# A decoder layer on one core: the FFN unit's steps within a slot, and who makes x1 at the end

## What is computed

```python
x = x + attn(ln(x))      # 32 query heads, 8 key/value heads of 128, rope, causal softmax;
                         # q, k, v, o weights are (codes - 8) * scales, scales per 128 rows
q1 = clip(round(ln(x) / s1 + z1), 0, 255) - z1          # fake_quant, times s1
q2 = clip(round(ctx / s2 + z2), 0, 255) - z2            # ctx: 2 x 1024 x 1024, times s2
x = x + (q1 @ q2) * (s1 * s2)
bw = mean(|w|, row) * sign(w) - clip(w, -1, 1) + clip(w, -1, 1)   # in this order, 1024 x 1024
x = x + ln(x) @ bw.T
```

## Time and profile before

| | |
|---|---|
| runs | 1189.84, 1192.79, 1192.4 us; median 1192.4 |
| profiled execution | 1189.75 us, its span 1188.0 us |
| busy | PE 1111.0 (94%), DVE 925.9 (78%), ACT 656.9 (55%), POOL 594.1 us (50%) |
| mean granted TensorE clock | 0.986 |
| chain that ended last | PE 82%, DVE 11%, issue 2%, ACT 2% |

### The profile page before, as it was taken

The page is one execution under the profiler, slowest core; times in us unless marked ns, Lnnn a source line. Parts: engine busy times, 40 slices in busy tenths (PEclk is TensorE's granted clock), DMA queues, the critical chain, the costliest instruction groups (busy, mean ns, idle before and its releaser), DMA issues.

```text
span 1188.0 us, 19387 instructions
## 1 busy us (share of the span) xinstructions
PE 1111.0 (94%) x5924; PEld 552.8 (47%) x5924; DVE 925.9 (78%) x1491; ACT 656.9 (55%) x1454; POOL 594.1 (50%) x692
## 2 busy tenths in 40 slices
PE   3799999789999999999999999999999998769998
PEld 2334444345545445545544545444454453435553
DVE  6867531358988878888888888999999988788773
ACT  2344432466677767767767776666666664223320
POOL 0112000477676766767767677776777765200000
PEclk9999999999999999999999999999999999899999
DMA  7344552176766757667576676666767754600111
GB/s 252 107 126 119 177 149 82 27 153 146 159 151 145 166 127 158 149 139 164 139 158 145 144 165 130 153 145 148 150 146 143 161 108 95 179 1 19 35 38 52
DMA packets 283186, 152.94 MB, mean 129 GB/s; under 512 B 229216, under 2 KB 241760, under 8 KB 283104
## 3 DMA queue, kind: packets, MB, share of 16 engines
q1 hardware_dynamic: 275328, 138.60, 50.3%
q10 hardware_dynamic: 7776, 13.37, 4.0%
HBM read 93.19 MB, written 4.19 MB: 82 GB/s over the span
## 4 chain that ended last, share of the span: by engine, by line
PE 82%; DVE 11%; issue 2%; ACT 2%; DMA 1%; POOL 1%; SPq 0%; ACTq 0%; DVEq 0%; POOLq 0%
PE side_ps L523 9%; PE side_ps L525 9%; PE side_ps L524 9%; PE proj_ps L655 8%; PE out_ps L655 8%; PE side_ps L634 7%; PE proj_ps L523 6%; PE proj_ps L524 6%; PE proj_ps L525 6%; PE score_ps L617 2%; PE score_ps L620 2%; PE score_ps L621 2%; PE score_ps L766 2%; DVE x_acc L1386 2%; DVE x_acc L1395 1%
## 5 line engine op out<-in xcount | busy, mean ns | idle before, releaser
L523 PE MATMUL side_ps<-hT,w_a 128*128 128x512 f16 x512 | 195.7, 382 | 13.5 <-DVE rot L1311 13.5
L1110 POOL TENSOR_TENSOR w_b<-prob,w_b 128x896 f16<-128x896 f32 (+2 forms) x192 | 188.6, 996 | 37.2 <-ACT w_b L942 37.2
L1098 POOL TENSOR_TENSOR swapped<-swapped,sin_t 128x512 f32<-128x512 f32 x80 | 102.1, 1276 | 194.2 <-ACT swapped L857 194.2
L524 PE MATMUL side_ps<-hT,w_a 128*128 128x512 f16 x512 | 195.4, 382 | 0.0
L525 PE MATMUL side_ps<-hT,w_a 128*128 128x512 f16 x512 | 195.3, 381 | 0.0
L1386 DVE SCALAR_TENSOR_TENSOR x_acc<-proj_ps,o_now,x_acc 128x1024 f32<-128x1024 f32 x116 | 148.0, 1276 | 53.2 <-PE proj_ps L655 53.2
L1103 POOL TENSOR_SCALAR prob<-prob,row_inv 128x512 f32<-128x512 f32 (+3 forms) x256 | 170.8, 678 | 17.7 <-DVE row_inv L1468 10.9
L915 ACT ACTIVATE prob<-score_ps,neg_max 128x512 f32<-128x512 f32 (+3 forms) x256 | 132.2, 519 | 60.6 <-DVE neg_max L1361 27.1
L1117 POOL TENSOR_TENSOR q_sb<-rot,q_sb 128x512 f16<-128x512 f32 x64 | 74.1, 1158 | 173.1 <-ACT q_sb L907 173.1
L1386 DVE SCALAR_TENSOR_TENSOR x_acc<-out_ps,o_now,x_acc 128x1024 f32<-128x1024 f32 x116 | 147.4, 1271 | 0.0
L942 ACT ACTIVATE w_b<-prob 128x896 f16<-128x896 f32 (+2 forms) x192 | 99.6, 552 | 54.6 <-POOL prob L1103 49.9
(11 more groups left out here) (188 smaller groups left out, 2140.0 us busy)
## 6 DMA issues: line engine op xcount, KB each, us to landing
stage_c<-in_codes_dram SPq DMA_DIRECT2D x96, 256.0 KB, 2.8
stage_s<-in_scales_dram SPq DMA_DIRECT2D x96, 256.0 KB, 3.8
stage_o<-in_codes_dram SPq DMA_DIRECT2D x64, 256.0 KB, 3.8
ctx_raw<-in_ctx_dram ACTq DMA_DIRECT2D x32, 256.0 KB, 3.3
x_acc<-in_x_dram SPq DMA_DIRECT2D x8, 512.0 KB, 9.3
prob<-in_ffn_w_dram ACTq DMA_DIRECT2D x16, 256.0 KB, 2.9
work<-w_b SPq DMA_TRANSPOSE x256, 3.0
hT<-in_x_dram SPq DMA_DIRECT2D x8, 512.0 KB, 5.1
```

The lines of the kernel that those rows point to most:

```text
L523: pe.matmul(o, stat(0), mov(0), start=first, stop=False)
L524: pe.matmul(o, stat(0), mov(1), start=False, stop=False)
L1098: pool.tensor_tensor(swapped[:, :], swapped[:, :], sin_t[:, :], ALU.mult).then_inc(done, 1)
L1110: ins = pool.tensor_tensor(prob16[:, 1, to:to + w], prob[:, at:at + w], prob16[:, 0, to:to + w], ALU.subtract)
```

## The change

Four edits.

1. In every slot with an FFN unit, `wf_clip` goes ahead of `q_lo` and `norm` on GpSimd, `wf_sign` ahead of `prob_split` part 0 on ScalarE, and `wf_difference` between `o_add` 1 and `o_add` 2 on VectorE.
2. Slot 62 is now an ordinary slot. Head 30's eight units all stand in slot 63 as `o_unit` and `o_add`; only head 31 has `two_units` and `add_two`. ScalarE runs part 1 of `prob_split` and `o_cut` ahead of `ao_part` in slot 63.
3. The column parts go to ScalarE (Identity with scale and bias, a new column of `scal`). Tile 0's x1 is still added from PSUM by VectorE, and its stats and root run alone. Tiles 1 to 7 are copied from PSUM by ScalarE (`y_copy`) and added to the input by GpSimd (`x1_add`). The transposes of tiles 4 and 5 stand between `turn_i1(0)` and `cross(0)`, those of 6 and 7 behind it.
4. Clip and rounding of tiles 2 to 7 leave VectorE: GpSimd clips (`x1_clip`), ScalarE adds the rounding constant (`x1_round`), and `x1_sum` takes it off again.

```diff
@@ TensorE, slot
-                if known(p) and p == N_SLOTS - 2:
+                if known(p) and p == N_SLOTS - 1:
                     scores(p, i, g, 0)
                     o_unit(p - 1, prev[1], 3)
                     scores(p, i, g, 1)
                     o_unit(p, i, 0)
+                    o_unit(p, i, 1)
                     scores(p, i, g, 2)
-                    for k in range(1, UNITS):
-                        o_unit(p, i, k)
+                    o_unit(p, i, 2)
+                    o_unit(p, i, 3)
                     for k in range(UNITS):
-                        two_units(NH - 2, 0, k)
-                    weigh(p - 1, prev[1], prev[0])
-                    return
-                if known(p) and p == N_SLOTS - 1:
-                    for u in range(3):
-                        scores(p, i, g, u)
-                        two_units(NH - 2, 1, u)
-                    two_units(NH - 2, 1, 3)
+                        o_unit(N_SLOTS, 0, k)
                     column_sums(0, 0)
                     weigh(p - 1, prev[1], prev[0])
                     return
@@ TensorE, the end
             for k in range(UNITS):
-                two_units(NH - 1, 1, k)
-            for t in range(TB, TT):
-                turn_y(t)
+                two_units(1, k)
             turn_i1(0)
+            turn_y(4)
+            turn_y(5)
             cross(0)
+            turn_y(6)
+            turn_y(7)
@@ ScalarE, slot
+                if known(p) and wf_early(p) is not None:
+                    wf_sign(wf_early(p))
                 prob_split(p, 0)
...
                 if has_ahead:
                     q_swap(p + Q_AHEAD)
-                if known(p) and wf_early(p) is not None:
-                    wf_sign(wf_early(p))
+                if known(p) and p == N_SLOTS - 1:
+                    prob_split(p, 1)
+                    o_cut(p, i)
+                    column_part(0, 0)
+                    ao_part(p - 1, i - 1)
+                    return
@@ ScalarE, new steps
+            def column_part(b, h):
+
+                act.wait_ge(col_summed, b * NB + h + 1)
+                act.activation(cc[:, b, h * S:(h + 1) * S], col_ps(b, h), ACT.Identity, scale=scal[:, 6:7],
+                               bias=scal[:, 10:11]).then_inc(cc_ready, 1)
+
+            def y_copy(t):
+
+                act.wait_ge(y_turned, t + 1)
+                act.activation(x1_rows(t), o_banks[t % 2][:, :, :].rearrange("p h (k t) -> p (h k) t", t=P), ACT.Copy)\
+                    .then_inc(y_copied, 1)
+
+            def x1_round(t):
+
+                act.wait_ge(x1_clipped, t - 1)
+                act.activation(xn[t % 2], xn[t % 2], ACT.Copy, bias=ROUND).then_inc(x1_rounded, 1)
@@ ScalarE, the FFN loop
                 if more:
                     x1_scale(t + 2)
+                if more:
+                    x1_round(t + 2)
                 if t:
                     h3_part(t)
@@ GpSimd, slot
+                    if known(p) and wf_early(p) is not None:
+                        wf_clip(wf_early(p))
                     if not (known(p) and p >= N_SLOTS - 1):
                         pool.wait_ge(q_done, p + 1)
                         q_lo(p + 1)
...
-                    if known(p) and wf_early(p) is not None:
-                        wf_clip(wf_early(p))
@@ GpSimd, the end
+            def x1_add(t):
+
+                pool.wait_ge(y_copied, t)
+                pool.wait_ge(xs_landed[t], 16)
+                pool.tensor_tensor(x1_rows(t), x1_rows(t), by_block(xs[:, t, :]), ALU.add).then_inc(x1_ready, 1)
+
+            def x1_clip(t):
+
+                pool.wait_ge(x1_scaled, t + 1)
+                pool.tensor_scalar(xn[t % 2], xn[t % 2], QMAX, 0.0, ALU.min, ALU.max).then_inc(x1_clipped, 1)
+
+            for t in range(1, 4):
+                x1_add(t)
+            for t in range(4, TT):
+                x1_add(t)
+                x1_clip(t - 2)
+            x1_clip(TT - 2)
+            x1_clip(TT - 1)
@@ VectorE, slot
                 if has_o:
                     o_add(p, i, 1)
+                if known(p) and wf_early(p) is not None:
+                    wf_difference(wf_early(p))
+                if has_o:
                     o_add(p, i, 2)
                 if has_ahead:
                     q_cos(p + Q_AHEAD)
-                if known(p) and wf_early(p) is not None:
-                    wf_difference(wf_early(p))
@@ VectorE, the FFN loop
                 if t:
                     y_part(t - 1, 0)
-                if more:
-                    x1_quant(t + 2)
```

More of the change, by code:

```diff
@@ L338, in build @@
         y_turned = sem("y_turned")
+        x1_first = sem("x1_first")
+        y_copied = sem("y_copied")
         x1_ready = sem("x1_ready")
@@ L1070, in _ @@
             wf_upper(WF_UNITS - 1)
-            next_roots(2)
+            column_part(0, 1)
+            column_part(1, 0)
+            y_copy(1)
+            next_roots(1)
+            y_copy(2)
+            y_copy(3)
             ao_part(N_SLOTS - 1, SLOTS - 1)
             x1_scale(0)
+            column_part(1, 1)
+            x1_sum(0)
+            next_roots(1)
             x1_scale(1)
-            x1_sum(0)
+            i1_T_part(0)
             x1_sum(1)
-            i1_T_part(0)
+            for t in range(TB, TT):
+                y_copy(t)
             i1_T_part(1)
@@ L1370, in o_scales @@
                 if last is not None:
-                    j, of = NH - 1 + last, (NKV - 1, RF - 2 + last)
+                    j, of = last, (NKV - 1, RF - 1)
                 dve.tensor_copy(o_now[:, of[1] % 2, :],
@@ L1413, in slot @@
                 n = p + FIRST_PIECES
-                if known(p) and p == N_SLOTS - 2:
-                    j = o_scales(g, i, 0)
+                if known(p) and p == N_SLOTS - 1:
+                    j = o_scales(g, i)
                     maxima(p, i, 0)
-                    q_sum(p + 1)
                     o_add(p - 1, i - 1, 3)
                     maxima(p, i, 1)
+                    dve.wait_ge(o_now_ready, j)
                     o_add(p, i, 0)
```

121 lines of the change are left out of this document (51 added, 70 removed).

## The result

| | before | changed |
|---|---|---|
| runs | 1189.84 to 1192.79; median 1191.4 us | 1173.84 to 1176.75; median 1175.6 us |
| ratio to before | | 0.9866, 95% interval 0.9846 to 0.9886 |
| profiled execution, its span | 1189.75, 1188.0 us | 1173.84, 1172.0 us |
| busy PE, DVE, ACT, POOL | 1111.0, 925.9, 656.9, 594.1 us | 1106.4, 904.1, 671.7, 621.7 us |

The change makes the kernel faster by 15.8 us; the prediction said 13.0 and 1179.4 us. Of the 3.8 us between 1179.4 and 1175.6, 1.0 is the base: the forecast started from the median of three runs, 1192.4, and with the fourth it is 1191.4. The sign, the sum of the end and the ceiling of the FFN stage were right. The slots gave more than their terms, and the experiments show that most of it came with GpSimd's clip, a move that the prediction had priced at nothing.

The account below looks back on a forecast made before the run. TensorE was taken as the bound, with 34.6 us of idling as the ceiling. FFN slots 3.6, first slots 1.2, end 8.2 and FFN stage 0 sum to 13.0 us, from 1192.4 to 1179.4 us; range 1173.5 to 1188.

Parts of the forecast that it names:

- The three stretches: First eight slots, FFN slots, and last two slots to first FFN product: idle TensorE of 6.5, 4.1 and 24.0 us.
- FFN slots, 3.6 us: Slots with an FFN unit: TensorE's nine waits for q_sum, together 4.0 us, go nearly wholly, gaining 3.6 us.
- The difference in the idle time ahead of o_add 2: FFN slots: VectorE's wf_difference, 0.94 us, fills 0.97 us of idling, so the next q_sum comes 0.4 us earlier.
- First slots, 1.2 us: First slots: slot 1's q_sum starts 0.8 us earlier and one more 0.43 us wait goes; bounds 0 and 3.
- The end, 8.2 us: Last two slots to the first FFN product: turn_h3(0) at 1058.7 instead of 1066.87, 8.2 us earlier.
- The table load: Ahead of tile 0's root on ScalarE: load now waits behind y_copy(1) and adds 1.28 us before the root.
- GpSimd's clip, taken at 1.85 us: FFN stage: GpSimd's clip of 1024 elements takes 1.85 us, between 1.44 and 2.52, and just fits.
- rival (a): FFN stage: a slow GpSimd clip makes it wait 0.6 us a tile, giving 1182.4 us; chance 0.15.
- The FFN stage at nothing: FFN stage: TensorE still bounds it and the new clip and rounding chain just fits, costing 0.
- (b): Slots: the moves give nothing because ao_part or the sine becomes the next wait, giving 1184.2 us; chance 0.14.
- (c): End: ScalarE's extra copies knot the queues, 8.2 us shrink to 1 or 2, giving 1185.6 to 1186.6; chance 0.08.
- (d): Slots: the early sign waits for a late wf_lower and slows the kernel; 1.85 us delay gives 1196; chance 0.03.

Follow-up runs that it names:

- e10: The kernel before with only GpSimd's clip moved ahead of q_lo and the norms: 1184.1 us, ratio 0.9948.
- e6: The changed kernel with three of GpSimd's x1 adds held back by waits: 1172.5 us, ratio 0.985.
- e12: The changed kernel with the old order of clip, sign and difference in every slot, and slot 63's difference behind the last o_add: 1185.4 us, ratio 0.9953.
- e2: The kernel before with only the slots' new order of clip, sign and difference: 1181.9 us, ratio 0.9923.
- e11: The kernel before with only ScalarE's sign moved ahead of prob_split: 1202.8 us, ratio 1.0107.

## Why the prediction was right, and where not

- **What bounds, and the ceiling.** The three stretches named from the earlier trace rows are those that got shorter, and nothing else did. Of the 34.6 us of idle TensorE, 12.9 went by the same rows (1.8, 4.1 and 7.0). The gain is larger than that, since an idle time listed between pipelined matmuls is shorter than what the wait costs; the next point has the numbers.
- **FFN slots, 3.6 us: the term was too small, and the named move the smaller part.** 6.7 us were measured. Two steps failed. The first is the price of a wait. The nine listed waits were priced at their listed 0.44 us; but a matmul is shown as 0.38 us long and follows its forerunner after 0.22, so each listed wait hides 0.16 more. By the starts of the slots, the nine slots with a wait are 0.6 to 0.7 us longer than in the changed kernel, 5.5 us together. The other slots from 40 on are longer by up to 0.2 without a listed wait, 0.6 us in sum, and another 0.6 lies between slot 7 and slot 40. The second is where the waits came from. The slots alternated between 12.71 and 12.17 us, in the trace of before, and now take 12.115 each; the prediction did not ask for the difference between the two kinds. Its step "GpSimd's clip moves ahead of q_lo ... Both cost nothing" was true of the cost and blind to the gain (e10: 5.6 us).
- **The difference in the idle time ahead of o_add 2** did what was said: it stands straight behind o_add 1, at 0.47 us instead of 0.94, as GpSimd's sine no longer runs beside it, and ao_rest waits for ao_part as forecast. On top of the early clip it is worth 1.2 us, since behind that TensorE is nearly the bound already.

```profile
831.05 0.47 DVE L1388 SCALAR_TENSOR_TENSOR w_b<-w_b,wf_mean 128x256 f32<-128x256 f32 x1
832.13 1.28 DVE L1445 SCALAR_TENSOR_TENSOR x_acc<-proj_ps,o_now,x_acc 128x1024 f32<-128x1024 f32 x1 [0.61 <-PE proj_ps L659]
833.33 0.69 DVE L1362 TENSOR_TENSOR side_ps<-side_ps,cos_t 128x512 f32<-128x512 f32 x1
834.38 0.69 DVE L1461 SCALAR_TENSOR_TENSOR work<-side_ps,work 128x512 f16<-128x512 f32 x1 [0.37 <-ACT work L952]
```

- **First slots, 1.2 us with bounds 0 and 3:** 2.0 over all kernels, 2.9 between these two traces; inside the bounds.
- **The end, 8.2 us: right, to the last 0.1 us by luck.** The first FFN transpose came 16.5 us earlier (the prediction had 13), 8.1 of them behind the start of slot 62. The sum held step by step as well: shifted by what the slots had gained (8.3), the last add of batch 0 was forecast at 1015.9 and ended at 1016.4; `x1_norm(0)` 1023.3, was 1022.63; `cross(0)` 1040.2, was 1040.57; `turn_h3(0)` 1050.4, was 1050.39. Errors of it cancel. From the last add to `x1_norm(0)` it had 7.4 us and 6.2 were measured: the copy from PSUM takes 1.03 and not 1.15 us, tile 0's transposes came at the full clock (1.09 and not 1.97 us), and VectorE's input to the root was ready only as the table load ended, so that the root waited for neither. From there to `cross(0)` it had 16.9 and 17.9 were measured, because `x1_quant(0)` was held, 2.0 us more. From `cross(0)` to `turn_h3(0)` it was 0.4 less. The chain of adds of slot 63 had two gaps of 0.40 and 0.32 us where a unit stood at the lower clock, which the prediction had named as what would speak against it; the forecast bore them.

```profile
1016.53 1.09 PE L742 MATMUL proj_ps<-ident,x_acc 128*128 128x128 f32 x8 [1.59 <-DVE x_acc L1454]
```

```profile
1018.54 1.03 ACT L1056 ACTIVATE x_acc<-out_ps 128x1024 f32<-128x1024 f32 x1 [7.57 <-PE out_ps L742]
1019.58 1.28 ACT L844 ACT_TABLE_LOAD   x1
1020.88 0.20 ACT L844 ACTIVATE root<-root 128x1 f32<-128x1 f32 x1
```

- **The table load.** It stands behind `y_copy(1)`, as forecast, and the root starts 1.30 us after it began; VectorE's input to the root was ready at 1020.84, so it cost nothing here and 0.8 in e6 and e12, where the transposes ran at the lower clock. The second load time that the prediction gave beside its sum, 2.66 us by the Trainium skill, "ScalarE: Activation LUTs", section "What ACT_TABLE_LOAD costs", is contradicted by this row too.
- **GpSimd's clip, taken at 1.85 us between 1.44 and 2.52: wrong, 1.04, below both bounds.** The rows of the bounds are the norms, which read a scale from SBUF, and the nearest one taken was the context's clip. The nearest by form stood in the same trace: the FFN unit's clip, two constants too, 256 elements in 0.40 us (0.39 in the row of 835.24), four of which are at most 1.6. By the Trainium skill, "GPSIMD Engine Reference", section "3.1 Elementwise — side-by-side cycle accounting", a body bound by its ports takes 1.03 cycles of 1.2 GHz an element; the estimate from it is 0.88 us for 1024 elements without the instruction's start. The trace agrees: from 256 to 1024 elements the clip grows from 0.40 to 1.04 us, 0.83 ns an element. So rival (a) was never near. ScalarE's rounding took 1.06 us.

```profile
1053.39 1.04 POOL L1221 TENSOR_SCALAR prob<-prob 128x1024 f32<-128x1024 f32 x1 [10.40 <-ACT prob L1066]
1054.40 2.36 POOL L1216 TENSOR_TENSOR x_acc<-x_acc,hT 128x1024 f32<-128x1024 f32 x1
```

- **The FFN stage at nothing:** it lost 0.5 us, in tile 1, where GpSimd's add at 1054.40 holds one of VectorE's sums:

```profile
1054.56 2.75 DVE L1568 SCALAR_TENSOR_TENSOR x_acc<-rot,scal,x_acc 128x512 f32<-128x512 f32 x1
1057.22 0.74 DVE L1568 SCALAR_TENSOR_TENSOR x_acc<-swapped,scal,x_acc 128x512 f32<-128x512 f32 x1
```

  The prediction had GpSimd's adds "off this path" and priced them only as GpSimd's own time. What they cost is VectorE's time, here and at `x1_quant(0)`: it had cited that the two engines share their interfaces for GpSimd's slowing down and not looked at the other side.
- **Rivals.** (b), the moves in the slots give nothing, is excluded by e2; (c) by the 8.1 us above; (d) became real only in e11, with the clip and not wf_lower as what the sign waited for. VectorE's busy time fell by 21.8 us, about as said.

## What to carry to other kernels

Where two engines alternate in a hand-written order, compare the duration of one form of instruction across its places: a form that takes 0.15 us in one slot and 0.62 in another, or 0.69 and then 2.71, may be held by a neighbour: look at what runs beside it in both places. Moving the neighbour's instruction by a few hundredths of a microsecond is then a change of its own. Price what the new work on GpSimd does to VectorE, not only how long GpSimd takes. And where equal slots take unequal times, find the instruction that differs before pricing a move by the listed waits.
